# Nucleus-sampled graph attention: one bisection fewer in step zero, casts moved to GpSimd, logits issued between products

## The reference

```python
for s in range(STEPS):                     # STEPS = 2
    A = _adj_from_feats(Xa, W1, W2, W3)    # 3327 x 3327
    Xf = Rf @ Xf                           # S = adj + I, rows normalised
    Xb = Rb @ Xb
    Xa = A @ Xa
    Z = Z + (Xf @ U1[s] + Xb @ U2[s] + Xa @ U3[s])
```

## Time and profile before

| | |
|---|---|
| median of 3 runs | 2577.81 us (2575.78 to 2578.23) |
| profiled execution, its own time | 2577.75 us |
| its span in the profile | 2576.0 us |
| VectorE busy | 2227.2 us, 86% |
| TensorE busy | 2014.6 us, 78% |
| ScalarE busy | 1680.0 us, 65% |
| GpSimd busy | 962.6 us, 37% |
| first masking pass of step zero to first subtraction of step one | 414.9 to 1396.9 us |
| chain that ended last | VectorE 21%, issue 9%, ScalarE 8%, GpSimd 7%, TensorE 4% |

### The profile page before, as it was taken

How to read it: one execution, slowest core, us unless ns; L and a number is a source line. 1 busy time by engine, 2 the same in 40 slices (tenths; PEclk the granted TensorE clock), 3 DMA queues, 4 the chain that set the end, 5 groups by cost and what they waited for, 6 DMA issues and landing times. The chain is left out here.

```text
span 2576.0 us, 33332 instructions
## 1 busy us (share of the span) xinstructions
PE 2014.6 (78%) x9898; PEld 1339.5 (52%) x9898; DVE 2227.2 (86%) x6888; ACT 1680.0 (65%) x1780; POOL 962.6 (37%) x1282
## 2 busy tenths in 40 slices
PE   2999465888888888888855887888888788888883
PEld 1555223566556665556633555555655555565552
DVE  6777658899889988889849999999999999999996
ACT  4334156788778877788636776777677677767730
POOL 1000042444434444344414354444535444453524
PEclk9999787999999999999976888888888888888896
DMA  6777210111111110111042000101010010101013
GB/s 226 286 284 271 92 44 17 47 45 36 41 43 47 47 45 31 42 47 46 32 156 80 19 19 19 38 19 38 19 38 19 22 35 19 37 20 37 18 61 121
DMA packets 65717, 167.54 MB, mean 65 GB/s; under 512 B 7037, under 2 KB 45307, under 8 KB 61947
## 3 DMA queue, kind: packets, MB, share of 16 engines
q1 hardware_dynamic: 65530, 165.43, 18.6%
HBM read 117.95 MB, written 47.45 MB: 64 GB/s over the span
## 5 line engine op out<-in xcount | busy, mean ns | idle before, releaser
L1348 PE MATMUL banks<-xa,pt 128*128 128x256 f32 x2704 | 660.2, 399 | 84.7 <-ACT pt L917 84.7
L893 ACT ACTIVATE junk_a<-pb_all,minus_t 128x3327 f16<-128x3327 f32 x151 | 463.5, 3069 | 261.5 <-POOLq L823 261.4
L1348 PEld LDWEIGHTS banks<-xa,pt 128*128 128x128 f32 x2704 | 527.8, 201 | 177.7 <-ACT pt L917 106.1
L1392 PE MATMUL banks<-region,at 128*128 128x512 f16 x2028 | 468.0, 392 | 0.0
L898 ACT ACTIVATE junk_a<-pb_all,minus_t 128x3327 f16<-128x3327 f32 x151 | 463.2, 3068 | 2.8
L1312 PE MATMUL banks<-keys,qs 64*128 64x512 f32 (+1 forms) x832 | 217.4, 642 | 221.8 <-DVE pb_all L1210 182.0
L808 POOL TENSOR_SCALAR over<-over,points 128x1 f32<-128x1 f32 x151 | 57.4, 380 | 821.7 <-ACT junk_a L898 821.6
L917 ACT ACTIVATE pt<-banks 128x896 f32<-128x896 f32 x208 | 178.0, 857 | 240.4 <-PE banks L1340 240.4
L1392 PEld LDWEIGHTS banks<-region,at 128*128 128x128 f16 x2028 | 205.8, 102 | 245.3 <-issue 28.7
L1312 PEld LDWEIGHTS banks<-keys,qs 64*128 64x128 f32 x832 | 83.6, 222 | 360.8 <-DVE pb_all L1210 264.5
L1210 DVE TENSOR_SCALAR_CACHE_REDUCE pb_all<-banks 128x1024 f32<-128x1024 f32 x260 | 208.9, 848 | 62.1 <-PE banks L1312 59.9
(11 more groups left out here) (225 smaller groups left out, 3309.2 us busy)
## 6 DMA issues: line engine op xcount, KB each, us to landing
at<-adjT_d SPq DMA_DIRECT2D x52, 832.0 KB, 4.9
region<-in_adj_dram SPq DMA_DIRECT2D x25, 1663.5 KB, 8.0
adjT_d<-at SPq DMA_DIRECT2D x26, 832.0 KB, 3.9
fb_d<-fb_sb SPq DMA_DIRECT2D x26, 256.0 KB, 2.0
region<-fb_d SPq DMA_DIRECT2D x2, 3328.0 KB, 19.2
y_d<-y_sb SPq DMA_DIRECT2D x50, 128.0 KB, 1.7
x_d<-pb_all SPq DMA_DIRECT2D x1, 3328.0 KB, 10.4
qs<-q_d SPq DMA_DIRECT2D x104, 32.0 KB, 4.2
```

The source lines that it names most:

```text
L893: nc.scalar.activation(junk_a[:, 0:w], pb[u][:, 0:w], ACT.Relu, scale=sign, bias=t, accum_out=over[u][:, 0:1])\
L1348: last = nc.tensor.matmul(bank[4][:, 0:D], pt[sl][:, t * P:(t + 1) * P], xa[:, t0 + t, :], start=(t0 + t == 0), stop=(t0 + t == T - 1))
L1392: last = nc.tensor.matmul(bank[5 + n][:, :], at[i.slot][:, t, :], mov, start=(t == 0), stop=(t == T - 1))
```

## The change

Step zero: `BISECTIONS` goes from 5 to 4, so VectorE makes one full-width test instead of two for each tile (three instead of four in the first tile, where ScalarE makes one); `AIM` goes from 12 to 6 and `SORTED` from 32 to 24, so one sorting round of four goes. The two casts and the scaling for `fb_sb` go from ScalarE to GpSimd, in front of its two subtractions; they wait for `xfb` (VectorE's `spread`) and the store of the tile before. Step one: all sixteen removals are in order, and VectorE subtracts all 3327 columns; `below_late` and `kept_late` go with their waits. Both steps: while products of tile k are made, the first pair of logits of tile m is issued before the third product group, the second before the fourth; the other two follow the last.

```diff
-    BISECTIONS = (5, 3)
+    BISECTIONS = (4, 3)
-    AIM = (12.0, 12.0)
+    AIM = (6.0, 12.0)
-    SORTED = (32, 64)
+    SORTED = (24, 64)
...
                     if first and k.inside(T):
-                        pool.wait_ge(S2("fb_hi")[k.slot], 3 * (k.use + 1))
+                        pool.wait_ge(S2("xfb")[k.slot], 2 * (k.use + 1))
+                        pool.wait_ge(S2("fb_stored")[1 - k.slot], 16 * (k + 1).use)
+                        ch.add(nc.gpsimd.tensor_copy(fb_sb[:, 0:D], xf_sb[k.slot][:, :]))
+                        ch.link(nc.gpsimd.tensor_scalar(xk_sb[:, :], xb_sb[k.slot][:, :], kappa[:, :], None, ALU.mult))
+                        ch.link(nc.gpsimd.tensor_copy(fb_sb[:, 2 * D:3 * D], xk_sb[:, :]))
                         nc.gpsimd.tensor_tensor(fb_sb[:, D:2 * D], xf_sb[k.slot][:, :], fb_sb[:, 0:D], ALU.subtract)\
...
-                    if not first and i.inside(T):
-                        pool.wait_ge(S("below_late"), i.t + 1)
-                        late = pb[i.third][:, LATE:N]
-                        nc.gpsimd.tensor_tensor(late, late, below[:, LATE:N], ALU.subtract).then_inc(S("kept_late"), 1)
...
-                    if first and k.inside(T):
-
-                        fb = fb_sb
-                        act.wait_ge(S2("xfb")[k.slot], 2 * (k.use + 1))
-                        act.wait_ge(S2("fb_stored")[1 - k.slot], 16 * (k + 1).use)
-                        nc.scalar.activation(fb[:, 0:D], xf_sb[k.slot][:, :], ACT.Copy).then_inc(S2("fb_hi")[k.slot], 1)
-                        act.wait_ge(S2("fb_lo")[1 - k.slot], 2 * (k + 1).use)
-                        nc.scalar.activation(xk_sb[:, :], xb_sb[k.slot][:, :], ACT.Copy, scale=kappa[:, :]).then_inc(S2("fb_hi")[k.slot], 1)
-                        act.wait_ge(S2("fb_hi")[k.slot], 3 * k.use + 2)
-                        nc.scalar.activation(fb[:, 2 * D:3 * D], xk_sb[:, :], ACT.Copy).then_inc(S2("fb_hi")[k.slot], 1)
...
-                        for g in [*range(LATE_SEGMENTS, G), *range(LATE_SEGMENTS)]:
+                        for g in range(G):
                             d = below[:, g * W8:(g + 1) * W8]
...
-                        ch.add(nc.vector.tensor_tensor(p[:, 0:LATE], p[:, 0:LATE], below[:, 0:LATE], ALU.subtract))
+                        ch.add(nc.vector.tensor_tensor(p, p, below[:, 0:N], ALU.subtract))
...
-                def logits(j):
+                def logits(j, first_pair, end):
...
-                    for c, (c0, w) in enumerate(LCH):
+                    for c, (c0, w) in list(enumerate(LCH))[first_pair:end]:
...
-                            if c == 1 and not first:
-                                pe.wait_ge(S("kept_late"), k.t + 1)
...
                         for c in range(NT):
                             if c + 1 < NT:
                                 transposes(c + 1)
+                            if c >= 2 and m.inside(T):
+                                logits(m, c - 2, c - 1)
                             product(c)
                     if m.inside(T):
-                        logits(m)
+                        logits(m, 2 if k.inside(T) else 0, len(LCH))
```

More of the change, by code:

```diff
@@ L97, in gnn_program @@
     fill = {}
-    LATE_SEGMENTS = SEGMENTS[1] // 2
-    LATE = LATE_SEGMENTS * ((N + 1) // SEGMENTS[1])
     FEW_ROUNDS = 8
@@ L1009, in search @@
                     tg = targets[i.third][:, :]
-                    if not first and not (i.static and i.t == 0):
-                        dve.wait_ge(S("kept_late"), i.t)
                     main = ch
@@ L1131, in search @@
                     else:
-                        for g in [*range(LATE_SEGMENTS, G), *range(LATE_SEGMENTS)]:
+                        for g in range(G):
                             d = below[:, g * W8:(g + 1) * W8]
[L1134 to L1138, removed]
+                            ch.add(nc.vector.match_replace(d, rank[:, 8 * g:8 * g + 8], d, 0.0))
                         answer(i, 1)
                         ch.all_done()
-                        ch.add(nc.vector.tensor_tensor(p[:, 0:LATE], p[:, 0:LATE], below[:, 0:LATE], ALU.subtract))
+                        ch.add(nc.vector.tensor_tensor(p, p, below[:, 0:N], ALU.subtract))
                     links.setdefault(s, ch.count)
@@ L1229, in settle @@
                         ch.wait()
-                        if not first:
-                            dve.wait_ge(S("kept_late"), i.t + 1)
                         c2 = Chain(dve, "step_settle_1", base=5 * i.n)
```

## The result

The changed kernel takes 2615.48 us, median of 4 runs (2612.8 to 2616.78), against 2577.85 us for the kernel before in the same session: ratio 1.0155, 95% interval 1.0134 to 1.0175. It is slower by 38 us; the forecast was 2549 us, 28.8 us faster. The end of the range, 2587, was passed by 28 us.

The account below looks back on a forecast made before the run. Step zero was taken as bound by a ScalarE-TensorE loop of 34.0 us plus 1.4 of accidents, step one by VectorE. Middle tiles -24.0, first -4.4, last -2.9, subtraction +2.5 gave -28.8 us: 2549 us, range 2534 to 2587.

Parts of the forecast that it names:

- Where the cut pass falls: Step zero, VectorE: cut pass from 37.3 to 41.0+d after a tile's first pt, GpSimd's step asking at 42.3.
- d: Time GpSimd's casts take from VectorE per step-zero tile: 0.37 to 3.2 us, taken as 1.7.
- the loop of 33.98: Step zero, ScalarE and TensorE: 28.55 us from first pt to zt plus 5.43 to the next pt.
- 4.39 us of VectorE as freed: Step zero: one bisection less lets VectorE's following work start 4.39 us earlier.
- 39.2 us of waits for logits: VectorE's seven waits in step zero's middle tiles, claimed to go with logits issued between products.
- what would make me wrong: Listed signs: tiles over 35.4 with GpSimd's step under the cut pass, TensorE's clock falling, a second any_un reading.
- The accidents of the kernel before: Step zero: drifting tiles put GpSimd's step under VectorE's cut pass, 1.4 us a tile above the loop.
- L1007 runs 31 times: Sign in the profile after: VectorE's full-width bisection pass, forecast under line L1021, 31 times instead of 57.
- The whole subtraction: Step one: VectorE subtracting all columns takes 3.66 us, 0.10 more in each of 26 tiles, +2.5 us.
- rival (c): Step zero: 24 candidates don't reach and a tile falls to the slow search, +70 us; chance 0.02.
- Rival (a): Step zero: GpSimd's casts push the cut pass, tiles of 35.9 to 36.6 us, 2585 to 2602; chance 0.14.
- the half-way cases of the cut pass: Step zero: d between 2 and 2.9, tiles of 34.7 to 35.6 us, about 2567; chance 0.18.

Follow-up runs that it names:

- experiment 1: Changed kernel with VectorE's addition of z (add_z) in step zero moved behind the cut pass; 2586.41 us, ratio 1.0038.
- experiment 5: Changed kernel with fifteen TensorE filler products, result unread, behind step zero's flag count; 2597.51 us, ratio 1.0077.
- experiment 6: Changed kernel with add_z behind the cut pass and fifteen TensorE filler products behind the flag count; 2539.68 us, ratio 0.9852.
- experiment 10: Changed kernel with add_z behind the cut pass and all logits behind the last product; 2539.89 us, ratio 0.9861.
- experiment 2: Changed kernel with the two casts and the scaling of fb_sb back on ScalarE; 2615.55 us, ratio 1.0146.
- experiment 4: Changed kernel with eight TensorE filler products, result unread, behind step zero's flag count; 2616.8 us, ratio 1.0149.
- experiment 9: Kernel before with only the first two pairs of logits issued between the products; 2626.89 us median of 10 runs, no ratio given.
- experiment 3: Changed kernel with all four pairs of logits behind the last product group again; 2606.2 us, ratio 1.0111.
- experiment 8: Kernel before with only BISECTIONS, AIM and SORTED of step zero set as in the change; 2586.65 us, ratio 1.004.

## Why the prediction was wrong

**The step that failed** is "Where the cut pass falls". Counted from the `pt` that it collides behind, I put the pass at 3.3 to 7.0+d (37.3 to 41.0+d less the loop of 33.98), ahead of GpSimd's request at 8.3. It runs from 6.6 to 10.3, over the request. The first pass isn't to blame: it began 5.5 us before that `pt`, where I had it 3.7 before. What was wrong is the stretch behind it: I let VectorE run from that pass into the cut pass, over `add_z`, which waits for the keys copy of ScalarE, 5.1 us after the *next* tile's `pt`. In the kernel before, the fifth pass lay over this wait, so its middle tiles showed none, and what shows no wait is easily taken for something that can't wait. Removing the pass uncovered it: 4.81 us. The order in the code and the offset of the copy would have given it: 5.1 for the copy, 0.1 until the addition starts, 0.4 for it and 1.0 for the small instructions are 6.6, and 6.6 to 10.3 covers 8.3. Experiment 1 shows the wait to be the cause, since moving that one addition brings ScalarE's wait from 2.99 to 1.16. I had counted 4.39 us of VectorE as freed; the wait is as large. The 39.2 us of waits for logits didn't go either: the list after has 49.9 us in 44 waits, which cost nothing, since VectorE waits another 2.5 us a tile for flags behind them.

**The second term, missing altogether,** is what TensorE does with flags that come early. I wrote that the logits between products free VectorE and priced nothing against that; a falling clock is named only under what would make me wrong, without a price and in no rival. The page before had a wait for `zt` in it, the 15.0 us above, which was to grow with each microsecond that the flags came earlier. The trace before had a price as well, in the tile from 984.23: TensorE waits 5.08 us, and its fourth product group takes 4.63 us instead of 2.43 at half the clock.

```profile
1001.84 4.63 PE L1348 MATMUL banks<-xa,pt 128*128 128x256 f32 x10 [5.08 <-ACT pt L917]
```

```profile
1003.00:1005.00 2.00, 2.00 (x7) 1.55 (x6) 0.00 (x0) 1.84 (x2) 0.07 (x1) 0.50 0.00 0
```

What it cost in the changed kernel is the 1.7 us a tile above. Experiments 5 and 6 show that it is the clock: with TensorE kept busy, the same products take 2.83 us.

**What held.** The loop of 33.98 us is real: 34.0 in experiment 6, 34.05 in 10. These two took 2540 us with both losses away, 9 us under the forecast of 2549. The accidents of the kernel before were what I said (GpSimd's step under the cut pass), and the change didn't remove them but locked nearly every tile into one, a shorter one: ScalarE waits 3.0 us in it, where it waited up to 4.6. L1007 runs 31 times. The first tile gained 2.3 us where I said 4.4, the last with the stretch behind it 2.3 where I said 2.9. The whole subtraction takes 3.62 us (3.66 forecast) and step one grew by 1.4 us (2.5 forecast):

```profile
L1123 DVE TENSOR_TENSOR pb_all<-pb_all,below x26: 3607/3620/3620, 1433.7 to 2552.4; 128x3327 f32<-128x3327 f32 x26
```

`any_un` is read 52 times again, so no tile took the slow search: rival (c) didn't happen.

**The casts.** Rival (a) gave the nearest time, 2585 to 2602, by a mechanism that plays no part. GpSimd's rows:

```profile
821.83 3.79 POOL L845 CAST fb_sb<-xf_sb 128x256 f16<-128x256 f32 x1 [0.32 <-POOL points L818]
825.61 1.03 POOL L846 TENSOR_SCALAR xk_sb<-xb_sb,kappa 128x256 f32<-128x256 f32 x1
826.71 0.40 POOL L847 CAST fb_sb<-xk_sb 128x256 f16<-128x256 f32 x1
827.19 0.68 POOL L848 TENSOR_TENSOR fb_sb<-xf_sb,fb_sb 128x256 f16<-128x256 f32 x1
```

The cast, the scaling and the subtraction unhindered are 0.40, 1.03 and 0.68, against my 0.45, 0.98 and 0.66. The first cast stands 3.79 us under VectorE's first pass. VectorE's small instructions beside the rest keep their lengths, but for one of 0.36 us that takes 0.22 in the first tiles. By the Trainium skill, "SBUF — State Buffer", section "SBUF: two separate sides", the second to start of two such instructions is locked out for the whole of the first. The trace agrees: the blocked one in this tile is GpSimd, 3.79 against 0.40 us. Small losses of VectorE do occur: in experiment 2, beside GpSimd's subtractions `fb_sb` around 823 us, two of its small instructions take 0.51 and 0.72 us, which are 0.24 and 0.22 in the changed kernel. Here they cost nothing, since VectorE waits behind them for `add_z` (3.94 us there, 4.81 in the changed kernel); with and without the casts the time is the same.

**The range** held the half-way cases of the cut pass, but each rival took one loss at a time. The two losses came together, 3.5 us above the loop in 20 tiles, where the kernel before paid 1.4 on average.

## What to carry to other kernels

Before counting an engine's time as freed, walk its own queue forward in the code from the freed instruction and ask of each wait that it passes when that semaphore comes, also of waits that the profile shows at zero: an addition of 0.4 us, standing in the wrong place, cost 29 us here. Work moved forward on TensorE can leave a hole further back, and a hole has a price when its clock falls; ask where the engine will stand idle, not only who gets the result sooner. And where tiles drift into and out of a collision, an edit of one engine's length sets the phase for all of them, and what is to be forecast is that phase. An edit that shortens the loop gains by the same road: the `zt` copies ahead of the exponentials were worth 37 us in the kernel before, most of it by collisions that went, and 58 us in the changed one once the addition was moved, of which 47 are had without them, by filling TensorE's gap or by moving the logits back (experiments 6 and 10).

## What the runs showed of the hardware

The clock of TensorE doesn't follow from the length of the wait ahead of it alone. After a wait of 1.96 us the twelve products took 4.51 us in experiment 4, after 2.08 us they took 2.83 in nearly all tiles of experiment 10 and 4.45 and 4.10 in two, and in experiment 9 some tiles had 2.83 after 3.77 us. Behind waits of 0.4 to 0.6 us they took 2.83 in each tile of experiments 3, 5, 6 and 8. The same holds for another group: ten products with `xa` took 4.63 us after 5.08 in the kernel before, and after 3.45 us in experiment 8 either 2.43 or 3.3 to 4.6. What else decides is open; it wasn't tried. The loss has a second size too: 5.46 us for the same products in experiment 1, after the same 3.77 us of waiting as in the changed kernel, with 4.51.

GpSimd's one-column step takes 0.27 us free, and under a full-width VectorE pass it takes what is left of that pass and little more: begun 1.72 us into a pass of 3.69, it took 2.10.
